# First attention's slots: GpSimd and ScalarE wait for VectorE's add of a buffer's old slot in place of TensorE's last product of it

## What is computed

```python
h = jnp.maximum(_layernorm(x, axis=-1), 0.0)
x = x + _L0_gnn_ref(h, src, dst, edge_weight, ...)    # twice (x + spmm) @ W, layer norm, gelu; then @ Wp
h = jnp.maximum(_layernorm(x, axis=-1), 0.0)
x = x + _L1_gnn_ref(h, W1, al1, ar1, W2, al2, ar2, src, dst)

def gat_conv(x, W, attn_l, attn_r, src, dst, n_nodes):
    H, D = attn_l.shape
    feat = (x @ W).reshape(n_nodes, H, D)
    el = jnp.einsum('nhd,hd->nh', feat, attn_l)
    er = jnp.einsum('nhd,hd->nh', feat, attn_r)
    e = jax.nn.leaky_relu(el[src] + er[dst], NEG_SLOPE)
    m = jax.ops.segment_max(e, dst, num_segments=n_nodes)
    ex = jnp.exp(e - m[dst])
    denom = jax.ops.segment_sum(ex, dst, num_segments=n_nodes)
    alpha = ex / denom[dst]
    out = jax.ops.segment_sum(alpha[:, :, None] * feat[src], dst, num_segments=n_nodes)
    return out.reshape(n_nodes, H * D)
```

## Time and profile before

| | |
|---|---|
| median of 3 runs | 3279.8 us |
| span of the profiled execution | 3272.4 us |
| TensorE busy, share of the span | 2624.1 us, 80% |
| VectorE | 2317.7 us, 71% |
| ScalarE | 1279.7 us, 39% |
| GpSimd | 1066.1 us, 33% |
| mean granted clock of TensorE | 0.930 of full |
| moved by DMA | 537.23 MB, 164 GB/s |

### The profile page before, as it was taken

How to read it: one execution, slowest core, us unless ns; L and a number is a source line. 1 busy time by engine, 2 the same in 40 slices (tenths; PEclk the granted TensorE clock), 3 DMA queues, 4 the chain that set the end, 5 groups by cost and what they waited for, 6 DMA issues and landing times.

```text
span 3272.4 us, 51000 instructions
## 1 busy us (share of the span) xinstructions
PE 2624.1 (80%) x17803; PEld 1952.4 (60%) x17803; DVE 2317.7 (71%) x3106; ACT 1279.7 (39%) x3089; POOL 1066.1 (33%) x1299
## 2 busy tenths in 40 slices
PE   5777777999899997285888888777677677876999
PEld 3666664545455554265777777555555555674888
DVE  7999997796334443288788787966666666785786
ACT  7888884020001112001444444444544454503443
POOL 3000000111102225530566666666666665003000
PEclk8999999999899998597999999899988999967999
DMA  4444446434477872031677766666666666061543
GB/s 134 183 181 177 167 182 240 123 113 134 143 262 255 261 253 89 15 106 53 181 194 193 198 190 184 179 186 186 184 184 189 184 184 190 12 200 54 158 155 112
DMA packets 316172, 537.23 MB, mean 164 GB/s; under 512 B 114066, under 2 KB 219044, under 8 KB 315668
## 3 DMA queue, kind: packets, MB, share of 16 engines
q1 hardware_dynamic: 244724, 308.43, 28.8%
q0 software_dynamic: 71200, 225.54, 24.7%
HBM read 419.84 MB, written 115.21 MB: 164 GB/s over the span
## 4 chain that ended last, share of the span: by engine, by line
PE 53%; DVE 28%; issue 7%; another core or an unknown queue 5%; ACT 5%; DMA 1%; POOL 1%; DVEq 0%; ACTq 0%; SPq 0%; POOLq 0%
PE ps L1718 20%; PE ps L1499 14%; PE ps L1706 8%; DVE a L590 8%; PE ps L1635 4%; DVE a L585 3%; DVE a L586 3%; PE ps L1405 2%; DVE a L1165 2%; DVE a L836 2%; ACT oht L1370 2%; DVE a L862 1%; ACT oh L1372 1%; PE ps L1633 1%
## 5 line engine op out<-in xcount | busy, mean ns | idle before, releaser
L1718 PE MATMUL ps<-a,oh 128*128 128x260 f32 x2008 | 508.8, 408 | 133.2 <-DVE a L1177 55.1
L1827 POOL DMA_INDIRECT a<-t,mid x502 | 486.7, 969 | 376.9 <-PE ps L1718 140.3
L1370 ACT ACTIVATE oht<-iota,mid 128x128 f32<-128x128 f32 x830 | 333.3, 402 | 627.0 <-PE ps L1718 396.4
L1499 PE MATMUL ps<-a 128*128 128x512 f32 x1200 | 555.4, 602 | 13.4 <-DVE a L769 13.4
L1718 PEld LDWEIGHTS ps<-a,oh 128*128 128x128 f32 x2008 | 389.7, 201 | 233.7 <-ACT oh L1372 97.3
L1165 DVE TENSOR_TENSOR a<-a,ps 128x520 f32 x415 | 286.3, 690 | 290.3 <-PE ps L1718 193.5
L1718 PE MATMUL ps<-wts,oh 128*128 128x260 f32 x1312 | 342.8, 416 | 115.2 <-DVE wts L1177 42.7
L1466 PE MATMUL ps<-a 128*128 128x200 bf16 x1568 | 320.4, 255 | 108.7 <-issue 51.1
L1827 POOL DMA_INDIRECT wts<-t,mid x328 | 313.5, 956 | 178.8 <-issue 82.9
L1718 PEld LDWEIGHTS ps<-wts,oh 128*128 128x128 f32 x1312 | 261.4, 206 | 184.4 <-ACT oh L1372 77.6
L1499 PEld LDWEIGHTS ps<-a 128*128 128x128 f32 x1200 | 218.8, 192 | 221.8 <-issue 215.4
(11 more groups left out here) (329 smaller groups left out, 3910.5 us busy)
## 6 DMA issues: line engine op xcount, KB each, us to landing
a<-at_d SPq DMA_DIRECT2D x60, 1280.0 KB, 6.1
at_d<-a SPq DMA_DIRECT2D x49, 800.0 KB, 3.3
mt_d<-a SPq DMA_DIRECT2D x49, 800.0 KB, 4.9
a<-mt_d SPq DMA_DIRECT2D x30, 1280.0 KB, 6.1
a<-trlo_d SPq DMA_DIRECT2D x49, 512.0 KB
ot_d<-a SPq DMA_DIRECT2D x49, 320.0 KB, 5.9
a<-ot_d SPq DMA_DIRECT2D x49, 256.0 KB, 3.3
a<-t,mid POOLq DMA_INDIRECT x502
```

The costliest lines, as they stand in the source:

```text
L1370: e.activation(oht[:, k, :], iota[:, :], ACT.Abs, bias=ndl[:, k, s:s + 1]).then_inc(*own.inc())
L1499: m = e.matmul(acc[f].rearrange("p (x d) -> p x d", x=8), X[:, hi, P * f:P * (f + 1)], a, start=(hi == 0), stop=end, skip_group_check=True)
L1718: t = e.matmul(pbig[b][:, 512 * u:512 * u + 260], oh[:, so, k, :], hrows[2 * r + k][:, 260 * u:260 * (u + 1)], start=(k == 0), stop=(k == 1))
L1827: e.indirect_dma_start(out=hrows[2 * r + k], out_offset=None, in_=t2, in_offset=bass.IndirectOffsetOnAxis(ap=srci[:, k, s:s + 1], axis=0)) ...
```

## The change

In `gather_heads` GpSimd waits for `head_add` in place of `head_mm`, with the same count: VectorE's add of the slot that used the buffer last, in place of TensorE's product of it. In ScalarE's loop over slots the wait before the one-hot pair is changed in the same way. Further, in the aggregation, both waits for a register's value now go through a register into which the larger of that value and 1 is written first; the value waited for is the same where it is 1 or more, as it is by its `min_val`. Nothing that is computed changes.

```diff
--- before.py
+++ after.py
@@ -1277,6 +1277,7 @@
 
 
             ereg = [e.alloc_register(f"ae{i}") for i in range(4)]
+            ends = e.alloc_register("pair_end")
             e.wait_ge(*V("regs"))
             for p in range(NPAIR):
                 if p % 4 == 0:
@@ -1286,7 +1287,8 @@
                     e.wait_ge(at_out[u], 32 * (p // 16))
                 pair = bank(p % 8)[:, 0:2 * W2].rearrange("p (w n) -> p w n", w=2)
                 o = stage[:, u, :, :].rearrange("p k (h v) -> p k h v", h=NB)[:, :, :, 8 * w:8 * w + 8].rearrange("p k h (w d) -> p w (k h) d", w=2)
-                e.wait_ge(slot_done, e.snap(ereg[p % 4], min_val=1, max_val=S))
+                e.reg_alu(ends, ereg[p % 4], 1, ALU.max)
+                e.wait_ge(slot_done, ends)
                 e.activation(o, pair.rearrange("p w (h d) -> p w h d", h=2 * NB), ACT.Copy).then_inc(window_out, 1)
                 e.wait_ge(window_out, p + 1)
                 e.activation(pair, bc(mzero[:, :].rearrange("p (a b) -> p a b", a=1), [P, 2, W2]), ACT.Copy).then_inc(window_free, 1)
@@ -1362,7 +1364,7 @@
                 so = s % 4
                 for k in range(2):
                     if s >= 4:
-                        e.wait_ge(head_mm, s - 3)
+                        e.wait_ge(head_add, s - 3)
                     elif s == 0 and k == 0:
                         e.wait_ge(*V("slots2"))
                     if s or k:
@@ -1442,6 +1444,7 @@
             for i in range(8):
                 e.matmul(bank(i), ones[0:1, :], zrow, start=True, stop=True).then_inc(window_free, 1)
             breg, freg = [], []
+            free = e.alloc_register("free_at")
             for s in range(S):
                 b, i = divmod(s, SB)
                 k, w = divmod(s, P)
@@ -1459,7 +1462,8 @@
                     e.wait_ge(*V("weighted", b))
                 if i % 8 == 0:
 
-                    e.wait_ge(window_free, e.snap(freg[s // 8 % 4], donate=True, min_val=1, max_val=NPAIR + 8))
+                    e.reg_alu(free, freg[s // 8 % 4], 1, ALU.max)
+                    e.wait_ge(window_free, free)
                 c = e.snap(breg[s % 4], donate=True, min_val=0, max_val=7 * 512 + W2)
                 g, z = divmod(i, SG)
                 lo = ohr[:, b % RB, g, :, z]
@@ -1822,7 +1826,7 @@
             def gather_heads(s):
                 r = s % NR
                 if s >= NR:
-                    e.wait_ge(head_mm, s - NR + 1)
+                    e.wait_ge(head_add, s - NR + 1)
                 for k in range(2):
                     e.indirect_dma_start(out=hrows[2 * r + k], out_offset=None, in_=t2,
                                          in_offset=bass.IndirectOffsetOnAxis(ap=srci[:, k, s:s + 1], axis=0)).then_inc(gh_in[r], 16)
```

## The result

| | before | after |
|---|---|---|
| time, median | 3279.59 us (3279.08 to 3279.99, 4 runs) | 3398.13 us (3393.43 to 3415.31, 4 runs) |
| ratio | | 1.037, 95% interval 1.0344 to 1.0396 |
| profiled span | 3272.4 us | 3391.6 us |
| mean granted clock | 0.930 | 0.902 |

The forecast was 3314.8 us, in a range that ended at 3345. The sign is right, the size is not: +119 us in place of +35.

What follows compares the result with a forecast made beforehand. The prediction took rounds of gathers, restarted by TensorE's held-up reports, to bound the late slots. Terms 0 + 35 + 0 + 0 + 0 gave 3307.4 us profiled, 3314.8 us median; range 3240 to 3345, the forecast's own 3290 to 3340.

Steps and rivals of the forecast that it cites:

- The bound of the late part: First attention's slots, 2120 to 2774 us: no engine full; TensorE's held-up semaphores start GpSimd's gather rounds, 2.92 us per slot.
- GpSimd's wait, late part, +35: First attention from 2120 us: gathers restart behind the add, lengthening rounds by 35 us, to 3.08 us per slot.
- The price of a restart: Late slots: each GpSimd restart comes 0.8 us later, the length of an add and the answer to the wait.
- The three fifths: Late slots: share taken of 58 us (72 waits by 0.8 us), giving +35 us; a choice, not a measurement.
- GpSimd's wait, first part, 0 with ends −40 and +20: First attention, 1570 to 2040 us: VectorE near its bound, GpSimd's 83 us left absorb later starts; cost 0.
- ScalarE's wait, 0: ScalarE's slot loop: one-hot pair still ready before VectorE's multiply ends, with 1.1 us of cover; cost 0.
- The sweeps, 0: Between the two stretches, some 20 slots: gathers slowed beside VectorE's sweeps are covered by GpSimd's slack; 0, uncovered +52 us.
- The registers, 0: Aggregation: extra register instructions, 3 us on ScalarE and 7 on TensorE, hidden behind VectorE; 0, uncovered +10 us.
- Faster: Rival on the slots: products freed sooner as gathers start behind the add; priced at −40 us, 3240 us, chance 0.27.
- absorbed: Rival on the slots: restart is later, but gather flow sets the round, or waits effectively no later; 3280 us, chance 0.23.
- Slower by more: Rival on the slots: the whole 58 us plus 24 us for TensorE's slots at a lower clock; 3362 us, chance 0.08.
- Slots A to D: Four late slots TensorE issues from 2256.66 us in 7.51 us; C's release claimed held up while gathers move.

Runs made afterwards that it cites:

- the gate: Kernel before with changed register waits, TensorE also waiting every fourth slot until later gathered rows land: 3646.74 us; with GpSimd's wait moved to the add, 3761.86 us.
- the run with traffic: Kernel before with changed register waits, plus a 128 KB DRAM-to-DRAM copy by SyncE beside each slot from slot 8 on: 3295.75 us on a slow chip.
- gp_only: Kernel before with changed register waits and only GpSimd's wait moved to VectorE's add: 2982.58 us against 2977.23 us for the kernel before, ratio 1.0019.
- act_only: Kernel before with changed register waits and only ScalarE's wait moved to VectorE's add: 2980.16 us against 2977.23 us for the kernel before, ratio 1.0011.
- regs_only: Kernel before with only the aggregation's two register waits changed: 2980.43 us against 2977.23 us for the kernel before, ratio 1.0010.
- whole: The changed kernel itself, run again on a quick chip beside the kernel before: 2983.28 us against 2978.64 us, ratio 1.0021.
- half_base: Kernel before with changed register waits, each gather from slot 10 on fetching 260 of 520 floats: 2978.95 us against 2977.37 us, ratio 1.0005.

## Why the prediction was right in sign and wrong in size

- **The bound of the late part: right.** Rounds started by TensorE's held-up reports, with GpSimd's restart as the place where the change bites.
- **GpSimd's wait, late part, +35: right, +33.5.** 3.08 us a slot as forecast. The price of a restart, 0.8 us, came out as 0.81 a round under the gate, but by two terms that the prediction did not have: the pause grew by 1.1 us and 0.3 came back. The three fifths were a choice. That both fit is partly luck: 58 us assumed 72 pauses that keep their number, and in slots 180 to 400 there were 69 of 1.67 us before and 46 of 3.15 us after.
- **GpSimd's wait, first part, 0 with ends −40 and +20: the failed step, +71.5 (+80.5 with slots 0 to 20).** It argued from busy time: VectorE 79% busy, so near its bound; GpSimd 387 of 470 us, so 83 us of room. But a mean over a stretch can't tell room from pauses that end at a wait on the very path that the change lengthens. The trace of before held two answers. GpSimd's waits in this stretch (96.0 us, put down to TensorE) are as many as in the late part. And of the 160 slots from 20 to 180, 145 have their first gather start before the end of the add that it was to wait for; in the late part it is 106 of 220. The upper end of +20 was "an add or two", where by the rows 65 pauses were to be priced. Even the late part's 0.8 us would have given 52 us. The rest was in VectorE's queue: the add stands behind a look read that has a held-up report of its own, and behind a multiply. The pauses behind a look read went from 1.6 to 4.0 us each and account for the whole +71.5.
- **ScalarE's wait, 0: nearly right.** +0.11% on a quick chip and +0.19% (0.07 to 0.31) on a slow one, some 6 us, in both with the register instructions.
- **The sweeps, 0: right.** Ten gathers of more than 1.5 us before, nine after, with 12.0 and 9.9 us in all above the usual 0.945. The sentence of the Trainium skill that I weighed there (SBUF — State Buffer, "SBUF: two separate sides") neither gained nor cost anything that the traces show. Its second half, by which nothing of the kind passes between TensorE and a DMA, agrees with the runs as far as bytes go: half of them (2.72 us behind the product), or more traffic (2.94), left TensorE's reports about where they were (2.77).
- **The registers, 0: right.** ScalarE's maximum takes 36 ns where the MOVE took 29, TensorE's 32 ns; VectorE's last one-hot product ended at 524.1 us after and 526.7 before, ScalarE's last clearing copy at 529.6 and 532.0. All register edits together cost 0.10% (0 to 0.19) on a quick chip.
- **Rivals.** "Faster" and "absorbed" both had GpSimd's restart move without cost, and they held half of the chance. "Slower by more" came nearest, but what it added to the late part's 58 us was 24 us for TensorE's clock. The clock did fall, from 0.98 to 0.91 in 1570 to 2040 us and from 0.91 to 0.83 in the late part; the late part still cost no more than without it, so this was not the cause there. Under the gate the loss came with almost the same clock in the first part (0.82 and 0.81) and a higher one in the late part (0.72 and 0.75). In the recorded pair its share of the first part wasn't separated.
- **What I couldn't have read:** that the rounds themselves belong to some chips. On a quick chip "absorbed" would have been the right answer, with +0.2%.

## What to carry to other kernels

Before a wait is moved to a later event, go through every stage in which that wait runs and compare, instruction by instruction, when the waiter started and when the new event came; each start that lies before it is to be priced, and a stage's busy share doesn't excuse one. The price is everything that stands in the signalling engine's queue ahead of the new event, with the waits in that queue, and not the event's own length. Where a resource is recycled in a ring, signal from the engine that really frees it; that the last reader's report is itself late is a reason to look at the chip, not to wait for someone further down.

## What the runs showed of the hardware that was not expected

- **The same kernel on six chips: 2977 to 2980 us on three, 3257 to 3274 us on three others.** Against the recorded trace of before a quick chip gets its first gather of the slots at 1380 to 1386 us (1432), needs 426 us for slots 20 to 180 (496), 537 us for slots 180 to 400 (647) and 462 us behind the last add (480); VectorE's last one-hot product of the aggregation ends at 524 to 527 us on both. Up to 1250 us, with some 340 instructions of GpSimd, the recorded before and the run with the registers alone stay within 3 us of each other. Of the 292 us between them 184 arise in the slots, 18 behind the last add and nearly all the rest between 1250 us and the first add.
- **TensorE's reports lag on the slow chips only.** Add behind the modelled end of its product, mean of slots 10 to 160: 0.80 us on a quick chip, 2.61 to 2.94 on slow ones with the old wait. Late part, maximum: 4.0 to 4.2 us against 7.3 to 7.4 with the old waits.
  An add can also be late by VectorE's own order, as the multiply of two slots on stands ahead of it: on the quick chip the mean of the late part is 2.70 us, though VectorE stood idle before one add of 220. The adds before which it did stand idle (over 0.3 us) are therefore the better measure. In the recorded before they are 85 in slots 180 to 400, 5.03 us behind in the median and 7.35 at most. Under the gate they are 101 and at most 0.54 us behind, on a quick chip and on a slow one.
- **The lag doesn't need a lower clock of TensorE.** Slots A to D of the prediction's round ran at a granted clock of 1.00 (2256.6 to 2264.2 us), and C's add came 7.4 us behind.
- **The lag follows neither bytes nor DMA load** (half the bytes: 2.72 us; share 0.79: 2.94 us). With the old wait, GpSimd goes on 1.3 to 1.5 us after the end of its last issue in the first part, in the median of 72 to 75 pauses, with whole and with half rows alike. This points to GpSimd's issuing rather than to the data. It is only argued: no run changed the number of issues or of rows, and on a slow chip with the gate 122 products ended beside issues without a lag. What holds a report up, and why a chip has it or not, stays open.
- **On slow chips about half of the semaphore records are missing from a trace** (21,940 events in the recorded before, 22,525 in the run with traffic, against 40,311 in the run with the registers alone on a quick chip), which is why so many waits there carry "remote"; in the traces of gp_only, act_only, regs_only, whole and half_base none does. Whether that and the lag have one cause was not tried.
  The Trainium skill (NOTIFIC — the notification-queue block, "7.1 Overflow: three behaviours, one of which stalls the engine") says that the block which writes such records can drop them when a queue is full and can hold up the engine that produces them when an internal queue fills; it adds that its own measurements never saw the marks of an overflow. Lost records and late reports on the same chips would fit that; no run here shows it, nor whether the lag is there when no events are recorded.
- None of the kernels was faster than the kernel before on its chip by more than its runs scatter.
